# Gate of a cross-attention kernel on one NeuronCore: halves of 400 rows against 512 rows and 288 turned rows

## The reference

```python
memory_proj = jnp.einsum('bme,de->bmd', memory, W_mem)
scores = jnp.einsum('bnd,bmd->bnm', hidden_states, memory_proj) / jnp.sqrt(jnp.float32(D))
attn = jax.nn.softmax(scores, axis=-1)
memory_context = jnp.einsum('bnm,bmd->bnd', attn, memory_proj)
gate_input = jnp.concatenate([hidden_states, memory_context], axis=-1)
gate = jax.nn.sigmoid(jnp.einsum('bnf,df->bnd', gate_input, W_gate) + b_gate)
fused = hidden_states + gate * memory_context
return _rmsnorm(fused, norm_w)
```

## Time and profile before

| what | value |
|---|---|
| device time, median of 3 runs | 306.37 us (304.49 to 307.09) |
| device time of the profiled execution | 304.79 us |
| its span in the profile | 303.0 us |
| PE busy | 291.5 us, 96% |
| DVE, ACT, POOL busy | 182.9, 157.0 and 7.9 us |
| moved by DMA | 50.47 MB |

### The profile page before, as it was taken

One profiled execution on the slowest core, in us unless ns is written; L12 is line 12 of the kernel. 1 busy time (PEld: TensorE's weight loads), 2 busy tenths in 40 slices (PEclk: granted clock), 3 DMA queues, 4 the chain that ended last, 5 costly groups with the idle time before them and its releaser, 6 DMA issues.

```text
span 303.0 us, 4514 instructions
## 1 busy us (share of the span) xinstructions
PE 291.5 (96%) x1658; PEld 279.6 (92%) x1658; DVE 182.9 (60%) x268; ACT 157.0 (52%) x226; POOL 7.9 (3%) x13
## 2 busy tenths in 40 slices
PE   8999999999999999999999999999999999799961
PEld 8999999898989989898998989999999999799961
DVE  3658455567585656758565535243267767758895
ACT  5628337463653936356393506534535666436540
POOL 0000000000000000000000000000000000700010
PEclk9999999999999999999999999999999999999995
DMA  7995382634938386483934012193243344225118
GB/s 261 416 396 169 127 323 77 198 110 150 284 97 273 119 255 204 129 279 90 297 124 158 11 61 70 31 409 133 69 142 90 118 138 136 74 75 183 60 54 270
DMA packets 21342, 50.47 MB, mean 167 GB/s; under 512 B 1728, under 2 KB 5568, under 8 KB 21328
## 3 DMA queue, kind: packets, MB, share of 16 engines
q1 hardware_dynamic: 19952, 49.07, 47.9%
q10 hardware_dynamic: 1376, 1.21, 1.2%
HBM read 47.00 MB, written 3.28 MB: 166 GB/s over the span
## 4 chain that ended last, share of the span: by engine, by line
PE 93%; POOL 2%; DMA 1%; DVE 1%; issue 1%; ACT 0%; POOLq 0%; DVEq 0%
PE ps L282 67%; PE ps L394 11%; PE ps L370 11%; PE ps L384 1%; POOL rms L935 1%; POOL rms_diag L940 1%; DMA acc<-xT 1%; PE ps L401 1%; PE ps L471 1%; DVE acc L876 1%; PE ps L307 0%; POOLq L54 0%; PE ps L310 0%; PE ps L313 0%; PE ps L462 0%
## 5 line engine op out<-in xcount | busy, mean ns | idle before, releaser
L282 PE MATMUL ps<-act_hi,w_hi 128*128 128x400 f32 (+1 forms) x324 | 97.3, 342 | 0.0
L282 PE MATMUL ps<-act_lo,w_hi 128*128 128x400 f32 (+1 forms) x324 | 96.8, 341 | 0.0
L282 PE MATMUL ps<-act_hi,w_lo 128*128 128x400 f32 (+1 forms) x324 | 96.5, 340 | 0.0
L282 PEld LDWEIGHTS ps<-act_hi,w_hi 128*128 128x128 f32 x324 | 59.7, 188 | 0.9
L282 PEld LDWEIGHTS ps<-act_hi,w_lo 128*128 128x128 f32 x324 | 60.4, 188 | 0.0
L282 PEld LDWEIGHTS ps<-act_lo,w_hi 128*128 128x128 f32 x324 | 60.3, 188 | 0.0
L698 DVE TENSOR_TENSOR w_lo<-w_stage,w_hi 128x1024 fp32r<-128x1024 f32 (+2 forms) x34 | 39.4, 1160 | 26.1 <-ACT w_hi L504 26.1
L504 ACT ACTIVATE w_hi<-w_stage 128x1024 fp32r<-128x1024 f32 x31 | 32.8, 1057 | 36.7 <-PE ps L282 36.3
L698 DVE TENSOR_TENSOR cn_lo<-cn_stage,cn_hi 128x1536 fp32r<-128x1536 f32 (+2 forms) x24 | 28.5, 1216 | 5.2 <-ACT cn_hi L523 5.2
L698 DVE TENSOR_TENSOR ct_lo<-ct_stage,ct_hi 128x1444 fp32r<-128x1444 f32 x16 | 25.8, 1654 | 0.5 <-ACT ct_hi L515 0.5
L601 ACT ACTIVATE pc<-ps,row_inv 100x512 f32<-100x512 f32 x8 | 5.5, 688 | 34.0 <-PE ps L394 34.0
(11 more groups left out here) (79 smaller groups left out, 357.7 us busy)
## 6 DMA issues: line engine op xcount, KB each, us to landing
ct_stage<-ctxT SPq DMA_DIRECT2D x16, 722.0 KB, 9.7
w_stage<-w_gate_mc SPq DMA_DIRECT2D x16, 512.0 KB, 3.5
cn_stage<-ctxN SPq DMA_DIRECT2D x8, 768.0 KB, 5.8
cn_stage<-ctxN SPq DMA_DIRECT2D x8, 512.0 KB
w_stage<-w_gate_x SPq DMA_DIRECT2D x8, 512.0 KB, 8.3
x_again<-xT SPq DMA_DIRECT2D x1, 3200.0 KB, 12.4
acc<-xT SPq DMA_DIRECT2D x6, 400.0 KB, 6.4
w_stage<-w_mem_t SPq DMA_DIRECT2D x4, 512.0 KB, 5.7
```

What stands on the lines that cost most here:

```text
L282: done = nc.tensor.matmul(o, wgt, stream[h][part], start=first and wgt is wh and part == 0, stop=last and wgt is wl)
```

## The change

- The memory half of the gate is cut at row 512 instead of row 400 (`STEPS`): tile 0 in both parts, then tiles 1 to 7 in rows 0 to 511, then tiles 1 to 7 in rows 512 to 799. There are 16 steps, n = 0 to 15, of 512 or 288 rows. The weights of each tile are loaded and split once and stay in SBUF; five more places hold them (`W_HOME`), three of them in `q_hi` and `q_lo`, which are free by then.
- The last step is one of 288 rows. Its x half is never saved: the last batch's `gate_x` works in 512 and 288 rows, leaves the 288 in bank 7, and the last step adds onto them. ACT takes that sigmoid straight from PSUM.
- The norm of the first 512 rows is made once, in groups of 128 rows, within steps 10 and 11; all four diagonals are now DVE's. Their outputs, 8 tiles of 512 rows, are two a step in DVE's steps 11 to 14.
- The last 288 rows leave by rows. PE turns 3 x 8 blocks of 96 rows x 128 features (`turn`), 21 of them after the last step and 3 at the very end; PE sums the squares with rows on partitions, GpSimd's power gives one factor per partition, and ACT and DVE each scale half of the 1024 features while copying out of PSUM. SP stores three blocks of 96 x 1024 in `out_rows`.
- WARM_UP is 27 instead of 34, and SP issues the two pieces of the first weights that ACT issued.
- The loops over batches' last pair, over mc tiles and over gate steps are written out.

```diff
-WARM_UP = 34
-GROUPS = ((0, NH), (NH, NH // 2), (NH + NH // 2, NH // 2))
+WARM_UP = 27
+FIRST, CHUNK = 512, 96
+ROWS2 = (R - FIRST) // CHUNK
...
+STEPS = [(0, 0, FIRST), (0, FIRST, R)] + [(t, 0, FIRST) for t in range(1, KD)] \
+    + [(t, FIRST, R) for t in range(1, KD)]
+LAST = len(STEPS) - 1
+END0 = STEPS.index((KD - 1, 0, FIRST))
+W_HOME = (2, 6, 0, 3, 4, 5, 1, 2)
+SPLIT_AT = {n: n + 2 for n in range(KD - 2)}
...
+        def gate_bank(n):
+            r0, r1 = STEPS[n][1:]
+            return bank(G2B + n % 2, r1 - r0) if n < LAST else bank(GLB, r1 - r0, P, r0 - FIRST)
...
             sp.dma_start(acc[:, 0, 0:H], xT[0:P, 0:H]).then_inc(x_first_in, 16)
-            sp.dma_start(w_stage[:, 0, C // 2:C], w_mem[0][:, C // 2:C]).then_inc(w_first_in[1], 16)
+            for i in range(2):
+                cols = slice(i * C // 2, (i + 1) * C // 2)
+                sp.dma_start(w_stage[:, 0, cols], w_mem[0][:, cols]).then_inc(w_first_in[i], 16)
             sp.dma_start(acc[:, 0, H:R], xT[0:P, H:R]).then_inc(x_in[0], 16)
+            sp.dma_start(w_stage[:, 0, C:WB], w_mem[0][:, C:WB]).then_inc(w_in[0], 16)
...
+            for k in range(0, KD, 2):
+                sp.wait_ge(out_done, k + 2)
+                sp.dma_start(out_v[:, k:k + 2, :], acc[:, k:k + 2, 0:FIRST]).then_inc(stored, 16)
+            for i in range(ROWS2):
+                sp.wait_ge(row_left, i + 1)
+                sp.wait_ge(row_right, i + 1)
+                sp.dma_start(out_rows[i * CHUNK:(i + 1) * CHUNK, :],
+                             row_out[:, i * D:(i + 1) * D]).then_inc(stored, 16)
...
+            def gate_mc(n, after=None, work=None):
+                t, r0, r1 = STEPS[n]
+                pe.wait_ge(w_lo_done, J_G2 + 1 + t)
+                if 2 <= n < LAST:
+                    pe.wait_ge(gate_summed, n - 1)
                 for k in range(KD):
...
+                    done = three([gate_bank(n)], w_tile(W_HOME[t], k), [(act_hi[:, k, r0:r1], act_lo[:, k, r0:r1])],
+                                 k == 0 and n < LAST, k == KD - 1, onto=n == LAST)
+                    if k == after:
+                        work()
...
+            for n in range(END0 + 2):
+                gate_mc(n)
+            gate_mc(END0 + 2, 4, mean_first)
+            gate_mc(END0 + 3, 4, inverse)
+            for n in range(END0 + 4, LAST + 1):
+                gate_mc(n)
+            pe.wait_ge(weighted, LAST)
+            turn(0, 0, KD - 1)
+            pe.wait_ge(out_done, KD)
+            turn(1, 0, KD - 1)
+            turn(2, 0, KD - 1)
+            pe.wait_ge(summed, LAST)
+            pe.wait_ge(late_squared, 1)
+            for i in range(ROWS2):
+                nc.tensor.matmul(late_mean(i), late_sums(i), mean_w[:, :], start=True, stop=False)
+                done = nc.tensor.matmul(late_mean(i), square[:, LAST % 2, i * CHUNK:(i + 1) * CHUNK], mean_w[:, :],
+                                        start=False, stop=True)
+            done.then_inc(late_mean_made, 1)
+            pe.wait_ge(weighted, LAST + 1)
+            for i in range(ROWS2):
+                turn(i, KD - 1, KD).then_inc(turned, 1)
...
+            for n in range(LAST + 1):
+                if n in SPLIT_AT:
+                    split_gate_w(SPLIT_AT[n])
+                if n == END0 + 1 or n == LAST:
+                    finish(n - 1)
+                    sigmoid(n)
+                else:
+                    sigmoid(n)
+                    if n > 0:
+                        finish(n - 1)
...
+            for n in range(END0 + 3, LAST):
+                gate_sum(n)
+                sum_squares(n - 1)
+                gate_times(n)
+                fuse(n)
+                if n == END0 + 3:
+                    dve.wait_ge(weighted, END0 + 1)
+                    dve.wait_ge(inv_made, 1)
+                while done < min(KD, 2 * (n - END0 - 2)):
+                    output(done)
+                    done += 1
+            sum_squares(LAST - 1)
+            gate_times(LAST)
+            fuse(LAST)
```

More of the change, by code:

```diff
@@ L445, in gate_mc @@
                 for k in range(KD):
-                    if first and slot == 0:
+                    if n == 0:
                         pe.wait_ge(mc_lo_done, k + 1)
-                    stream = [(act_hi[:, k, h * H + part.start:h * H + part.stop],
-                               act_lo[:, k, h * H + part.start:h * H + part.stop])]
-                    o = bank(G2B + (slot if psum is None else psum), part.stop - part.start, P, part.start)
-                    done = three([o], w_tile(slot, k), stream, k == 0, k == KD - 1)
@@ L452, in gate_mc @@
-                    if between is not None and k == between[0]:
-                        between[1]()
-                done.then_inc(gate_made, 1)
-            def mean_square(g, done_sums):
-                b0, n = GROUPS[g]
-                pe.wait_ge(summed, done_sums)
-                for i in range(n):
-                    at = (b0 + i) % NH * N
-                    done = nc.tensor.matmul(bank(MSB[g], 1, N, i), square_sum[:, b0 // NH, at:at + N],
-                                            mean_w[:, :], start=True, stop=True)
-                done.then_inc(mean_made, 1)
@@ new lines, in gate_mc, with mean_first, inverse @@
+                done.then_inc(gate_made, 1)
+            def mean_first():
+                pe.wait_ge(summed, END0 + 1)
+                for i in range(FIRST // P):
+                    done = nc.tensor.matmul(bank(6, 1, P, i), square_sum[:, i * P:(i + 1) * P], mean_w[:, :],
+                                            start=True, stop=True)
+                done.then_inc(mean_made, 1)
+            def inverse():
+                pe.wait_ge(diag_done, FIRST // P)
+                for i in range(FIRST // P):
+                    done = nc.tensor.matmul(bank(RIB, P, P, i * P), ones[:, :], rms_diag[:, i, :],
@@ new lines, in turn @@
+            def turn(i, t0, t1):
+                at = FIRST + i * CHUNK
+                for t in range(t0, t1):
+                    done = nc.tensor.transpose(bank(2 * i + t // 4, P, CHUNK, t % 4 * P), acc[:, t, at:at + CHUNK],
+                                               ident[:, :])
+                return done
+            for n in range(END0 + 2):
[4 more added lines that the diff above has]
+                gate_mc(n)
@@ L908, in _, with sum_squares @@
[L908 to L922 removed]
+            def sum_squares(n):
+                rows = square_sum[:, slice(*STEPS[n][1:])]
+                dve.wait_ge(squared, n + 1)
+                if n > 0:
+                    dve.wait_ge(summed, n)
+                nc.vector.tensor_tensor(rows, rows, square[:, n % 2, 0:rows.shape[1]], ALU.add).then_inc(summed, 1)
```

395 lines of the change are left out of this document (170 added, 225 removed).

## The result

| what | before | after |
|---|---|---|
| device time, median (20 runs each) | 305.93 us (304.49 to 307.14) | 306.72 us (304.76 to 307.56) |
| profiled execution | 304.79 us | 307.06 us |
| its span | 303.0 us | 305.3 us |
| PE busy | 291.5 us | 293.8 us |
| moved by DMA | 50.47 MB | 46.31 MB |

The ratio of after to before is 1.0038, with a 95% interval of 1.0020 to 1.0055: slower, by 0.4% or 0.8 us in the medians. The runs of both kernels fall into two groups: 10 of before at 304.5 to 305.7 and 10 at 306.2 to 307.1; 4 of after at 304.8 to 306.0 and 16 at 306.4 to 307.6. Before was profiled in its lower group and after in its upper one, so their difference of 2.3 us is more than the change's. The groups differ in TensorE's granted clock, averaged over a run: 0.990 to 0.991 in the 4 lower runs of after, 0.980 to 0.986 in the 16 upper ones.

The account below looks back on a forecast made before the run. PE's unbroken matmul path was taken as the bound. PE's 1.5 us gain and a shorter norm chain, given back by DVE's lag and the turns, summed to 305.1 us; 305.8 was forecast, 303.0 to 308.8 for 8 in 10.

Parts of the forecast that it names:

- the base: Time the 0.3 us change is added to: profiled 304.79 gives 305.1, median 306.37 gives 306.7; 305.8 was chosen between.
- The sum: All terms added on the profiled execution: span 303.3 us, or 305.1 with what lies outside, 0.3 over 304.79.
- the turns at 2.3 us: Tail: PE turns 21 blocks at 0.11 us each from 75.8 to 78.1 us into the gate stage.
- 0.4 for a fall of the clock: Tail: 0.4 us added for PE's clock falling in the middle of the turns and sums.
- the stores at 410 GB/s: Tail: the last row stores, 1.18 MB, take 2.9 us at 410 GB/s (3.6 at 330).
- the stall of 1.35 us: First norm in the gate stage: PE waits 1.35 us for the diagonals, against 1.65 before, with GpSimd's power at 2.41.
- DVE's lag: Gate steps from 11 on: a DVE round of 3.85 us against PE's 3.18 loses 2.4 us.
- The start, taken at 0: First real matmul: later issue and lighter load offset each other; bounds 0.5 us later to 0.4 earlier.
- rival C: Kernel start: with fewer idle matmuls the clock rises later, costing 1.9 us, time 307.7; chance 0.12.
- The pitch of 288 columns: Gate stage: 288-column matmuls start 133 ns apart (range 127 to 142).
- rival B: Tail: PE's clock falls to half before the turns begin, costing 2.9 us, time 308.7; chance 0.14.
- Rival D: Gate stage: DVE keeps up, with power at 0.85 us and rounds at 3.2; 3.5 us earlier, time 302.3; chance 0.17.

Follow-up runs that it names:

- first experiment: Kernel before with only the changed kernel's start (27 idle matmuls, all first loads from SP): 304.90 us beside 304.88, ratio 0.9995.
- last experiment: Kernel before with the first diagonals on DVE right behind the epsilon, DVE idle while GpSimd raises to the power: 303.96 us, ratio 0.9961.
- the new order on DVE: Changed kernel with DVE's two outputs of 512 rows moved ahead of the sum of squares in steps 11 to 14: 303.56 us, ratio 0.9948 to before.

## Why the prediction was wrong

The forecast was 305.8 us, 0.6 under the 306.37 then known of before, and the probabilities were for no change that can be told. The measured change is 0.8 us to the slower side, clear of noise; the median after, 306.72, is inside the range.

**The steps that failed** are two terms of the tail and the base. The sum took the turns at 2.3 us with 0.4 for a fall of the clock, and the runs showed 3.86 us from the first turn to the first sum behind them. It took the stores at 410 GB/s and they moved about 300. Up to the end of the span these are 2.7 us that the sum lacked. A third step, the stall of 1.35 us with a power of 2.41, failed the other way and hid 1.0 of it. And the sum itself said 0.3 slower; the choice of 305.8, between two bases, turned that into 0.6 faster than the median shown.

What was right is that PE's gain is given back by DVE's lag and the turns. In the sum's own terms, from the start of the stage:

- **The start, taken at 0**: right in the sum, by luck. The first experiment puts it between -0.3% and +0.2%, and the profiled stage began 0.33 us later. But the first real matmul came 0.62 us earlier, outside the bounds of 0.5 later to 0.4 earlier, and the first ones were 0.33 us apart, which I had named as a sign of being wrong. At 400 columns that is the 1.2 GHz level, though the windows print a granted clock of 1.00 there. So rival C's slow start was there, at 0.8 us over the first six matmuls instead of its 1.9, and the earlier data hid most of it.
- **The pitch of 288 columns, taken at 133 ns**: right, it is 134 (288.22 to 289.16, 7 pitches). By the Trainium skill, "TensorE: Matmul & The Clock Gate", section "Back-to-back issue gap", the rule for an isolated warm matmul gives 122.5, and the trace of this stream of matmuls disagrees here too.
- **The stall of 1.35 us and a power of 2.41 "as it stood"**: wrong, and it made the forecast too long. I read 2.41 for 4 columns and 0.85 for 2 as a matter of columns or of first use, and did not ask what ran beside it. In after DVE waits for the power instead of working next to it:

```profile
272.21 1.03 POOL L952 TENSOR_TENSOR rms<-rms,minus_half 128x4 f32<-128x4 f32 x1 [270.74 <-DVE rms L909]
273.28 0.88 DVE L887 TENSOR_SCALAR rms_diag<-ident,rms 128x128 f32<-128x128 f32 x4 [1.22 <-POOL rms L952]
```

  It takes 1.03 us, PE does not stall, and the stage is 72.3 us, not 73.2. The last experiment shows in the kernel before that the power's length hangs on what DVE does beside it. The power is not the whole of the stall, though: the diagonals were done 57.0 us into the stage, 0.9 before my 57.9, and PE came for them at 57.3, 0.7 after my 56.6.
- **DVE's lag of 2.4 us at a round of 3.85** (the terms listed add to 3.89): right. The round is 3.82, and the last sigmoid starts 2.4 us behind PE's last matmul. Mostly by the shorter power, step 14 is weighted 74.8 us into the stage, where I had 75.8: 1.0 less.
- **The clock, 0.4 us "for a fall in the middle of the turns"**: mis-sized. From the first turn to the first sum 3.86 us passed instead of 2.3 + 0.4, and from the first turn to the copies 1.4 more than in my sum. At full clock the price was right: in the new order on DVE that stretch is 292.38 - 290.05 = 2.33. By the test that I gave rival B, half clock before about 77, it came true: the clock fell at about 292.7, 75.5 us into the stage. It fell within the first microsecond of the turns, not before them, and was back at about 296, so the sums were not slower, and B's 2.9 us were too many. I had the row that showed a fall after a rest of this kind (1.18 beside 0.69) and the 2.6 us of rest, and should have given the fall more than the middle. B rested in part on the Trainium skill, "TensorE: Matmul & The Clock Gate", section "Part 4: PE-mode transpose", by which the full clock does not engage for transposes, as they do not count as busy in the same way. From 291.97 to 295.83 PE does nothing but turns, and the granted clock rises from 0.50 in the window 295 to 296 to 0.95 in the next; with idle matmuls ahead of them the turns run at 1.00 from end to end. As far as this can show, the trace disagrees.
- **The stores, 2.9 us at 410 GB/s**: mis-sized. The rate is about 300 GB/s, 3.9 us for 1.18 MB, and the flow thins out at its end, to 41 GB/s from 304.0 to 304.4. From the start of the copies to the end of the span 7.1 us pass against my 5.8, 1.3 more, though the flow began a little sooner after the copies than I had it (1.6 us against 1.9). The number for it stood in the windows of before, 330 GB/s at the same place, which I set aside because its runs were shorter. It was the better guide, and the experiments show that neither the cut nor the queue changes the rate.

Together: 0.33 for the start, -1.0 for the earlier step 14, +1.4 for the turns and what follows up to the copies, +1.3 for the stores make 2.0, and the span is 305.3 where I had 303.3. Rival C's time, 307.7, fell by experiment. Rival D, that DVE keeps up, was not so in this kernel, but its first half was in substance: the power took 1.03, where it had 0.85. Its second half is what the new order on DVE made true: 303.56, near its 302.3 with the stores' 1.3 added.

**The base.** I put the forecast between the sum on the profiled execution (305.1) and the one on the median (306.7). The new median of before, 305.93, lies there, so 305.8 stood for a forecast of before as well, and the 0.3 by which the sum lay over before was lost in it; against the 306.37 then known it even said faster. The direction of the sum, slightly slower, was right, but partly by luck: without the power's error it would have said faster.

**Open.** Why the kernel before has an upper group of runs as well is not shown: no profile here is of one. In the 31 runs of before beside the first experiment, the 6 at 306.4 to 307.1 have mean granted clocks of 0.981 to 0.983 and the 25 others 0.985 to 0.988, so it goes with the clock. But a fall in the tail alone does not set them apart, since the profiled run, of the lower group, has one too, at 294 to 295. Idle matmuls were not tried in that kernel. That in the 4 lower runs of after the clock stayed up in the turns is inferred from their mean clock and from the kernel with idle matmuls.

## What to carry to other kernels

Look at what an in-order engine does while it waits, before counting its busy time: DVE's round was 3.82 us because of a wait of 0.94, and work that was ready stood behind it; swapping them gave 0.9%, part of it through the clock. Here a rest of 2.5 us on TensorE ahead of the turns cost twice, once as a rest and once as half the clock afterwards; a rest of 0.8 us or one filled with idle matmuls did not. Before a time is carried over, see what ran beside it: the power's 2.41 us became 1.03. When a change has many parts, try each alone: the move of four diagonals from GpSimd to DVE gave 1.4 us by itself. Take the rate of the last stores from stores at the same place in the old trace, not from loads.

## What the runs showed of the hardware

- GpSimd's power on 4 columns took 2.41 us with DVE operations of 1.22, 0.57 and 0.57 us beside it and 1.02 to 1.03 us with DVE idle. On 2 columns it took 0.85 beside two DVE operations of 0.37.
- Forty bf16 matmuls of 128 columns, 2.41 us, kept the clock at 1.00 through the wait and the turns; without them, after 2.52 us of rest, the clock fell to 0.50 and the same turns took 4.07 instead of 2.50. With a rest of 0.82 us the clock held by itself through the turns.
- The clock came back from 0.50 when PE had done nothing but float32 turns of 96 rows since 291.97: 7 passes in the window 295 to 296 at 0.50, then 14 in the next at 0.95.
- Stores of 96 partitions, in runs of 4 KB or of 2 KB, from one queue or two, move 299 to 324 GB/s in the windows shown, with the DMA engines' share at about 1.0. A store from 128 partitions in the same kernel moves 395, and loads at the start of the kernel 410, both at the same share.
